# A transformer layer with a mixture of experts: experts' bias added inside its own jobs in the last half, and a new order of the tail

## The chip, the core and the metric

The kernel runs on one core of a Trainium2 chip. The engines named below are PE (TensorE, matrix products), PEld (its weight loads), DVE (VectorE), ACT (ScalarE), POOL (GpSimd) and SP (SyncE, which issues most transfers). The metric is the device time in microseconds. Three runs of the kernel before gave 788.24, 789.04 and 795.55 us, median 789.04 us. The profiled execution took 789.42 us, of which 787.6 us are its span, from the first to the last instruction.

## What is computed

The input is x of 4 batches, 1024 rows and 128 features; there are 16 heads of 8 features. Everything is float32. Cut to what matters:

```
x  = x + attention1(layernorm(x))                  # strictly causal, softmax of att * mask
n  = layernorm(x)
c  = attention2(rope(n)) @ out_proj_w.T + out_proj_b   # causal
x1 = layer_norm(n + c, ln1_w, ln1_b)
gates = softmax(x1 @ gate_w.T + gate_b)            # 8 experts
top 2 of the gates, not renormalised
e_i = x1 @ expert_w[i].T + expert_b[i]
moe = sum over the top 2 of gate_i * e_i
out = x + layer_norm(x1 + moe, ln2_w, ln2_b)
```

## The kernel before

**Tiling.** A batch is cut in two halves of 512 rows, a half in four tiles of 128 rows. Work named `p1` prepares the first attention of a batch, `p2` finishes it and prepares the second attention, `p3` finishes the second attention of a half and does the experts. In the names, `("p3", b, "e0", t)` is a piece of work: t is a tile (0 to 7) for `e0`, `e1` and `moe`, and a half (0 or 1) otherwise.

**Order.** A planner in the file, `schedule()`, fixes the order of all pieces at build time from tables of assumed durations (`JOB_TIMES`, `TURN_TIMES`). It fills three lists: BEFORE (ahead of the attention), DURING (between the attention's score and value products, by far the largest part) and AFTER (behind the last value product). Every engine walks through the same lists and executes its own share in that order, waiting on semaphores, so an early piece that has to wait holds up every later one on its engine. Pieces with a PE part are called jobs. In AFTER, jobs go round over seven PSUM banks, and PE may run ahead of the readers by up to seven jobs.

**What is in AFTER.** The rest of the first half of the last batch (tiles 0 to 3) and all of the last half (tiles 4 to 7), here called the lone half, `LAST_HALF = (1, B - 1, 1)`:

- `num` turns the numerators of one group of heads, `att` divides by the sums, `att_turned` turns the quotient (ACT copies it out), `out` is the output projection, and DVE adds the residual.
- `stats`, `root`, `centre`, `scale`: first normalisation of four tiles. DVE does the moments, the centring and the scaling, POOL the inverse root (L1535, L1536).
- `x1T` turns x1; `gate` is the gate product; `exp` and `pick0` to `pick3` make the matrix G of gates on DVE (with one exponential on ACT).
- `e0` and `e1`: the experts' products of one tile, 512 columns each. In AFTER, ACT multiplies a product by the gates (L1464) and DVE only passes on the semaphore, by `read_by_act`; for the `e0` jobs of the lone half DVE multiplies itself (L1627, `probs<-scores,G`). After `e1`, DVE adds the two (L1627, `psum<-probs`), and POOL's `moe` folds the sum in two steps and adds `x1b` (L1561 to L1563).
- `GT` turns G, and `bias` multiplies it by the 8 rows of experts' biases; DVE adds x1 to make `x1b`. `moe` waits for it.
- `x2` prepares the residual; `stats2`, `root2`, `centre2`, `scale2`, `store`: second normalisation of four tiles and one transfer of 256 KB.

A float32 product of 512 columns shows up in the trace as two PE instructions, and `e0` or `e1` is one such product, so two instructions.

`read_by_act` (in words): DVE waits until ACT has read the job's bank, and then counts the job as free. Banks are freed in the order of the jobs, so PE sees a job as read only when DVE has come to it in its own list.

## Time and profile before

| | us |
|---|---|
| median of three runs | 789.04 |
| profiled execution | 789.42 |
| its span | 787.6 |
| PE busy | 681.1 (86% of the span) |
| ACT busy | 648.1 (82%) |
| DVE busy | 395.9 (50%) |
| POOL busy | 322.9 (41%) |

Shares over the span say little about the last 50 us. There the attention is over, each engine is busy for only part of the time, and the end is set by a chain that goes back and forth between DVE, PE, ACT and POOL. The granted clock of PE is 1.00 or 0.50 of full speed in each stretch (2.4 and 1.2 GHz). Idle time of an engine off the chain costs nothing. Times given as 7xx.xx are positions in the span of the profiled execution.

### The profile page before, as it was taken

Reading aid. Unit: us, or ns where it says so; the run is one execution under the profiler, and the core shown is the slowest. Engines: PE = TensorE matmul, PEld = TensorE weight load, DVE = VectorE, ACT = ScalarE, POOL = GpSimd, SP = SyncE. Lnnn points to the kernel's source line nnn. Section 1 sums busy time; section 2 is a strip of 40 time slices with the busy share of each in tenths; the row PEclk is TensorE's granted clock in tenths of the full one; section 3 lists DMA queues with packets and bytes.
Section 4 is the critical chain, followed back from the end, with each engine's and each line's share of the span. In section 5 each row is a group of like instructions: output and inputs, shape, how many; then the busy total and the mean of one; then the engine's idle time right before and its main releaser. Section 6 shows DMA issues by size and latency. Waiting matters only on the chain. (4 is left out here: it accounts for less than half of the span.)

```text
span 787.6 us, 15418 instructions
## 1 busy us (share of the span) xinstructions
PE 681.1 (86%) x5568; PEld 259.9 (33%) x5568; DVE 395.9 (50%) x1062; ACT 648.1 (82%) x721; POOL 322.9 (41%) x635
## 2 busy tenths in 40 slices
PE   4798998988899989989897989989999789999853
PEld 2333333433234333233232333233333233233422
DVE  5355344456445453556244644574345765455573
ACT  1499997999899997999698889998889798888721
POOL 3162235323633434434553245532666314424334
PEclk9589998999999997999898999999999999999976
DMA  6848357535567432424455244423545451230100
GB/s 162 288 136 263 101 202 239 178 127 202 181 213 243 162 110 86 148 83 135 143 163 155 104 141 130 146 83 121 190 151 179 158 162 60 70 96 1 41 13 15
DMA packets 77142, 109.86 MB, mean 139 GB/s; under 512 B 13928, under 2 KB 28400, under 8 KB 77040
## 3 DMA queue, kind: packets, MB, share of 16 engines
q1 hardware_dynamic: 72944, 107.32, 42.8%
q10 hardware_dynamic: 4096, 1.33, 0.8%
q8 instruction: 46, 0.75, 0.4%
q14 instruction: 56, 0.46, 0.2%
HBM read 60.94 MB, written 47.68 MB: 138 GB/s over the span
## 5 line engine op out<-in xcount | busy, mean ns | idle before, releaser
L1504 ACT ACTIVATE probs<-scores,shift 128x1024 f32<-128x1024 f32 x576 | 601.4, 1124 | 80.2 <-PE scores L1309 73.7
L1580 POOL TENSOR_SCALAR_AFFINE_SELECT probs<-probs 128x256 f32<-128x256 f32 (+1 forms) x448 | 197.5, 458 | 379.8 <-ACT probs L1504 379.1
L1334 PE MATMUL acc<-probs,v 128*9 128x512 f32 (+3 forms) x3072 | 322.2, 508 | 10.7 <-ACT num L1429 9.5
L1309 PE MATMUL scores<-qs,ks 32*128 32x512 f32 (+3 forms) x1536 | 185.1, 434 | 41.0 <-ACT probs L1504 37.4
L1309 PEld LDWEIGHTS scores<-qs,ks 32*128 32x128 f32 x1536 | 83.1, 189 | 259.9 <-ACT probs L1504 175.0
L1334 PEld LDWEIGHTS acc<-probs,v 128*9 128x9 f32 x3072 | 59.1, 100 | 132.2 <-issue 72.9
L1627 DVE TENSOR_TENSOR prod<-side,G 128x512 f32<-128x512 f32 x48 | 33.1, 691 | 89.3 <-PE side L1275 79.3
L1275 PE MATMUL side<-we,x1T 128*128 128x512 f32 x100 | 58.6, 669 | 0.8 <-DVE x1T L1916 0.8
L1561 POOL TENSOR_TENSOR moe<-psum 128x256 f32<-128x256 f32 x32 | 24.4, 762 | 51.3 <-DVE x1b L1627 26.6
L1429 ACT ACTIVATE num<-acc 128x512 f32<-128x512 f32 x64 | 38.2, 596 | 5.3 <-PE acc L1334 5.2
L1536 POOL TENSOR_TENSOR rstd<-rstd,expo 128x4 f32<-128x4 f32 x32 | 33.4, 1044 | 2.7
L1660 DVE COPY xT<-side 128x512 f32<-128x512 f32 x22 | 15.2, 691 | 30.2 <-PE side L1148 30.1
L1675 DVE TENSOR_SCALAR part<-side,binqk 128x512 fp32r<-128x512 f32 x16 | 12.0, 751 | 31.4 <-PE side L1154 21.8
L1154 PE MATMUL side<-xT,win 128*128 128x512 f32 x32 | 20.1, 712 | 6.6 <-DVE part L1676 6.6
L1464 ACT ACTIVATE probs<-scores,G 128x128 f32<-128x128 f32 x40 | 11.0, 389 | 15.4 <-PE scores L1275 9.9
L1675 DVE TENSOR_SCALAR part<-side,bqk 128x512 fp32r<-128x512 f32 x12 | 9.0, 751 | 25.0 <-PE side L1154 25.0
L1635 DVE BATCH_NORM_STATS2 stats<-xrow 128x6 f32<-128x128 f32 x72 | 15.6, 279 | 11.8 <-DMA xrow<-in_x 9.5
L1275 PEld LDWEIGHTS side<-we,x1T 128*128 128x128 f32 x100 | 15.5, 195 | 16.1 <-issue 11.4
L1627 DVE TENSOR_TENSOR psum<-prod 128x512 f32<-128x512 f32 x24 | 17.7, 737 | 3.1
L1275 PE MATMUL scores<-we,x1T 128*128 128x512 f32 x28 | 17.4, 767 | 0.0
L1562 POOL TENSOR_TENSOR moe<-moe 128x128 f32<-128x128 f32 x32 | 15.8, 493 | 2.5
L1848 DVE TENSOR_SCALAR sfx<-side,sfx 128x128 f32<-128x128 f32 x28 | 9.8, 351 | 12.6 <-PE side L1235 8.4
(186 smaller groups left out, 602.4 us busy)
## 6 DMA issues: line engine op xcount, KB each, us to landing
ks<-k_dram SPq DMA_DIRECT2D x96, 256.0 KB, 4.1
q_dram<-part SPq DMA_DIRECT2D x64, 256.0 KB, 3.5
qs<-q_dram SPq DMA_DIRECT2D x64, 256.0 KB, 3.2
num_dram<-num SPq DMA_DIRECT2D x60, 256.0 KB, 3.3
k_dram<-part SPq DMA_DIRECT2D x30, 256.0 KB, 4.0
xrow<-in_x SPq DMA_DIRECT2D x16, 256.0 KB, 4.4
nat<-num_dram SPq DMA_DIRECT2D x15, 256.0 KB
rdenb<-rden_dram SPq DMA_DIRECT2D x15, 256.0 KB
```

What stands on the lines that cost most here:

```text
L1154: signal(pe.matmul(out[:, :], w[:, int(name == "k"), :], xT[a][:, a or j, :], start=True, stop=True), last)
L1275: signal(pe.matmul(out[:, :], x1T[i // TH][:, i % TH, :], we[:, first:first + HALF], start=True, stop=True), last)
L1309: ins = pe.matmul(dst, ks[u][r, kt // TH, (kt % TH) * P:(kt % TH + 1) * P], qs[u][r, q0:q0 + w], start=True, stop=not shifted)
L1334: ins = pe.matmul(acc[h * VW:h * VW + VC, q0:q0 + w], v9[V_OF[k]][:, kt, :, HG * hg + h], src, start=(s == 0), stop=last, skip_group_check ...
L1429: act.activation(num[gp % 2][:, :], acc[:, :], ACT.Copy).then_inc(acc_read, 1)
L1504: act.activation(dst, src, ACT.Exp, bias=shift[:, column(st):column(st) + 1], scale=SCALE).then_inc(probs_raw, 1)
L1536: pool.tensor_tensor(r, r, expo[:, 0:1].broadcast_to(list(r.shape)), ALU.pow).then_inc(root_ready[w], 1)
L1561: link(pool.tensor_tensor(moe[:, :, :], psum4[:, i % 2, 0:2, :], psum4[:, i % 2, 2:4, :], ALU.add))
L1562: link(pool.tensor_tensor(moe1[:, :], moe[:, 0, :], moe[:, 1, :], ALU.add))
L1580: ins = pool.affine_select(out=blocks, in_=blocks, compare_op=ALU.is_ge, fill=0.0, base=a - 1, pattern=[[0, blocks.shape[1]], [1, P]], cha ...
L1627: return dve.tensor_tensor(out, in0, in1, op)
L1675: link(dve.tensor_scalar(pt[:, c, 0, :], src, bias[:, c:c + 1], None, ALU.add))
```

## The change

BEFORE and DURING come out the same; only AFTER changes, and one more transfer is in the loads of weights. In parts:

1. **Bias inside the jobs.** In the lone half `GT` and `bias` are gone. Each of its eight `e0` and `e1` jobs gets a second product, a row of ones (one partition) by a row of 512 bias values, accumulated in the same bank. POOL's last addition takes x1 in place of `x1b`. A tile `be_row` of 4 KB in one partition holds the biases and is loaded with the weights.
2. **Numerators first.** While a `num` job is pending, the planner lets PE take no other job.
3. **Products in two places.** The products of a tile lie in `probs0` or `probs1` by the tile's parity. The `e0` job of tiles 6 and 7 (and in the code that of tile 5 as well: `i > TH`) waits for the sum of the tile but one, no longer for that of the tile before it.
4. **Second normalisation by pairs.** `stats2` to `store` of the lone half are split in A (tiles 4, 5) and B (tiles 6, 7), each with a transfer of 128 KB.
5. The planner models ACT's time of reading otherwise and may let DVE take other work first. This moves rows, too.

```diff
@@ all_turns @@
-        out[x("GT")] = [x("pick3"), x("bias", 1)]
-        out[x("bias")] = [x("GT"), last("moe", 2)]
+        if not alone:
+            out[x("GT")] = [x("pick3"), x("bias", 1)]
+            out[x("bias")] = [x("GT"), last("moe", 2)]
...
+            n = 2 if alone and t > TH else 1
+            out[("p3", b, "e0", t)] = [x("pick3"), ("p3", *((b, "e1", t - n) if t else (b - 1, "e1", T - 1)))]
...
+        if alone:
+            for c, t in (("A", TH + 1), ("B", TH + 3)):
+                out[x("stats" + c)] = [("p3", b, "moe", t)]
+                out[x("root" + c)] = [x("stats" + c)]
+                out[x("centre" + c)] = [x("stats" + c)]
+                out[x("scale" + c)] = [x("centre" + c), x("root" + c), x("x2")]
+                out[x("store" + c)] = [x("scale" + c)]
@@ schedule, behind the last point @@
-            x = next((x for x in pending if x[2] in PIECES and operands(x, t)), None)
+            nums = any(y[2] == "num" for y in pending)
+            x = next((x for x in pending if x[2] in PIECES and (x[2] == "num" or not nums) and operands(x, t)), None)
...
-            if begun and begun[0][1] <= t and ready(begun[0][0], t, NPOINT) and (x is None or left(begun[0][0]) > left(x)):
+            act = acts(begun[0]) if begun and by_act(begun[0][0]) else t
+            if begun and begun[0][1] <= t and ready(begun[0][0], t, NPOINT) and (x is None or (left(begun[0][0]) > left(x) and act <= t + 0.3)):
@@ SP @@
+                if name in ("storeA", "storeB"):
+                    n = 2 * b + i
+                    c = "AB".index(name[-1])
+                    sp.wait_ge(y_ready, n + 1 + c)
+                    ts = slice(2 * c, 2 * c + 2)
+                    sp.dma_start(rows_of(out_d, *rows_half(b, i))[:, ts, :], y_of(n)[:, ts, :]).then_inc(y_out[i], 16)
@@ PE @@
-                        signal(pe.matmul(out[:, :], x1T[i // TH][:, i % TH, :], we[:, first:first + HALF], start=True, stop=True), last)
+                        alone = (1, b, i // TH) == LAST_HALF
+                        ins = pe.matmul(out[:, :], x1T[i // TH][:, i % TH, :], we[:, first:first + HALF], start=True, stop=not alone)
+                        if alone:
+                            ins = pe.matmul(out[:, :], ones[0:1, :], be_row[:, first:first + HALF], start=False, stop=True)
+                        signal(ins, last)
@@ POOL, moe @@
-                        pool.wait_ge(side_free, done(("p3", b, "bias", i // TH)))
+                        if alone:
+                            pool.wait_ge(rows_ready[2], 2 * b + i // TH + 1)
+                        else:
+                            pool.wait_ge(side_free, done(("p3", b, "bias", i // TH)))
+                        added = (x1_of(2 * b + i // TH) if alone else x1b[i // TH])[:, i % TH, :]
@@ DVE @@
-                                dve.wait_ge(products_ready, b * T + i)
+                                dve.wait_ge(products_ready, b * T + i - ((1, b, i // TH) == LAST_HALF and i > TH))
+                    if name[-1] in "AB":
+                        c = "AB".index(name[-1])
+                        ts = range(2 * c, 2 * c + 2)
+                        if name[:-1] == "stats":
+                            dve.wait_ge(moe_ready, b * T + TH * i + 2 * c + 2)
+                            moments(3, y_of(n), 1, ts)
```

**PE, behind the first normalisation of the lone half.** `x1T1` is x1 of the lone half, `x1T0` that of the half before it, `G1` the lone half's gates. Before:

```order
L1275 MATMUL scores<-we,x1T0 128x512 x4
L1251 MATMUL scores<-ident,xrow0 128x128 x4
L1275 MATMUL side<-we,x1T0 128x512
L1257 MATMUL scores<-wg,x1T1 128x8 x4
L1275 MATMUL scores<-we,x1T1 128x512 x4
L1263 MATMUL scores<-ident,G1 8x128 x4
L1270 MATMUL side<-be,GT 128x128 x4
L1275 MATMUL scores<-we,x1T1 128x512 x4
```

And of the change, from the same place (the pair of L1310 and L1313 stands eight times in all; two are shown):

```order
L1310 MATMUL scores<-we,x1T0 128x512 x3
L1285 MATMUL scores<-ident,xrow0 128x128 x4
L1310 MATMUL scores<-we,x1T0 128x512
L1291 MATMUL scores<-wg,x1T1 128x8 x4
L1310 MATMUL side<-we,x1T0 128x512
L1310 MATMUL scores<-we,x1T0 128x512
L1310 MATMUL scores<-we,x1T1 128x512
L1313 MATMUL scores<-be_row,ones 128x512
L1310 MATMUL scores<-we,x1T1 128x512
L1313 MATMUL scores<-be_row,ones 128x512
```

Two experts' jobs of tile 3 moved from ahead of the gate product to behind it, the two rows of turned gates and bias are gone, and the eight jobs behind have twice the products.

**DVE, from the gate logits to the gates of the lone half.** `y` with `l2w` or `x2r` is the second normalisation of the half before it. Before:

```order
L1627 TENSOR_TENSOR gr<-gr 128x32
L1635 BN_STATS stats3<-y 128x6 x4
L1638 BN_AGGR mv3<-stats3 128x2 x4
L1627 TENSOR_TENSOR gmask<-gr,bars8 128x32
L1646 SCALAR_TENSOR_TENSOR y<-y,mv3,l2w 128x128 x4
L1990 TENSOR_REDUCE gsum<-ga 128x4
L1991 RECIPROCAL gsum<-gsum 128x4
L1627 TENSOR_TENSOR gmask<-ga,gmask 128x32
L1627 TENSOR_TENSOR G1<-gmask,gsum 128x32
L1652 SCALAR_TENSOR_TENSOR y<-y,rstd3,x2r 128x128 x4
```

Of the change:

```order
L1674 TENSOR_TENSOR gr<-gr 128x32
L1674 TENSOR_TENSOR gmask<-gr,bars8 128x32
L2050 TENSOR_REDUCE gsum<-ga 128x4
L2051 RECIPROCAL gsum<-gsum 128x4
L1674 TENSOR_TENSOR gmask<-ga,gmask 128x32
L1674 TENSOR_TENSOR G1<-gmask,gsum 128x32
```

The second normalisation of the earlier half left this place.

**DVE, the end of the program.** `xrow0` is the lone half's result. The last rows before:

```order
L1627 TENSOR_TENSOR psum4<-probs1 128x512
L1635 BN_STATS stats3<-xrow0 128x6 x4
L1638 BN_AGGR mv3<-stats3 128x2 x4
L1646 SCALAR_TENSOR_TENSOR xrow0<-xrow0,mv3,l2w 128x128 x4
L1652 SCALAR_TENSOR_TENSOR xrow0<-xrow0,rstd3,xrow 128x128 x4
```

Of the change:

```order
L1674 TENSOR_TENSOR psum4<-probs1 128x512
L1699 SCALAR_TENSOR_TENSOR y<-y,rstd3,x2r 128x128 x4
L1693 SCALAR_TENSOR_TENSOR xrow0<-xrow0,mv3,l2w 128x128 x2
L1699 SCALAR_TENSOR_TENSOR xrow0<-xrow0,rstd3,xrow 128x128 x2
L1682 BN_STATS stats3<-xrow0 128x6 x2
L1685 BN_AGGR mv3<-stats3 128x2 x2
L1693 SCALAR_TENSOR_TENSOR xrow0<-xrow0,mv3,l2w 128x128 x2
L1699 SCALAR_TENSOR_TENSOR xrow0<-xrow0,rstd3,xrow 128x128 x2
```

Between the last sum of products and the last moments there now stand eight instructions: the earlier half's scaling, and pair A's centring and scaling.

## Rows read from the trace of the kernel before

**Rows 1.** Chain that ended last, its end: start, duration in us, engine and work.
```profile
779.04 0.69 POOL moe L1561
...
780.82 0.88 DVE stats L1635 x4
...
781.72 0.39 DVE mv L1638 x4
...
783.79 0.35 DVE xrow L1652
```

**Rows 2.** Timeline, first part of the tail: start, us, engine, line, work [idle before].
```profile
739.29 0.31 DVE L1778 COPY tot<-scores 128x144 f32<-128x144 f32 x1 [3.77 <-ACT probs L1464]
...
745.23 0.69 DVE L1627 TENSOR_TENSOR xrow<-scores,xr 128x512 f32<-128x512 f32 x1
...
747.17 0.86 DVE L1635 BATCH_NORM_STATS2 stats<-xrow 128x6 f32<-128x128 f32 x4
...
750.70 2.14 DVE L1652 SCALAR_TENSOR_TENSOR xrow<-xrow,rstd,l1b 128x128 f32<-128x128 f32 x4
...
750.86 0.77 POOL L1561 TENSOR_TENSOR moe<-psum 128x256 f32<-128x256 f32 x1 [0.36 <-DVE psum L1627]
```

**Rows 3.** Timeline of PE from the last idle stretches on, same columns.
```profile
744.13 3.60 PE L1275 MATMUL scores<-we,x1T 128*128 128x512 f32 x8
...
752.98 1.09 PE L1251 MATMUL scores<-ident,xrow 128*128 128x128 f32 x4 [5.26 <-DVE xrow L1652]
753.86 1.91 PE L1275 MATMUL side<-we,x1T 128*128 128x512 f32 x2
755.57 1.72 PE L1257 MATMUL scores<-wg,x1T 128*128 128x8 f32 x8
757.14 5.82 PE L1275 MATMUL scores<-we,x1T 128*128 128x512 f32 x8
...
768.84 2.04 PE L1270 MATMUL side<-be,GT 8*128 8x128 f32 x8 [3.78 <-DVEq L1624]
770.82 5.82 PE L1275 MATMUL scores<-we,x1T 128*128 128x512 f32 x8
```

**Rows 4.** Stretches: busy us of each engine, granted PE clock, DMA share, GB/s.
```profile
36.00:44.00 8.00, 7.93 (x56) 2.23 (x56) 3.94 (x20) 6.57 (x8) 4.93 (x11) 0.50 0.69 204
...
761.00:762.00 1.00, 1.00 (x3) 0.28 (x3) 0.97 (x7) 0.00 (x0) 0.00 (x0) 0.77 0.00 0
```

**Rows 5.** Timeline of DVE from the logits to the gates, same columns as Rows 2.
```profile
757.79 0.18 DVE L1627 TENSOR_TENSOR gl<-scores,bg 128x32 f32<-128x32 f32 x1
...
760.89 0.87 DVE L1635 BATCH_NORM_STATS2 stats<-y 128x6 f32<-128x128 f32 x4
...
762.29 1.15 DVE L1646 SCALAR_TENSOR_TENSOR y<-y,mv,l2w 128x128 f32<-128x128 f32 x4
...
764.13 0.19 DVE L1627 TENSOR_TENSOR G<-gmask,gsum 128x32 f32<-128x32 f32 x1
...
764.35 1.14 DVE L1652 SCALAR_TENSOR_TENSOR y<-y,rstd,x2r 128x128 f32<-128x128 f32 x4
```

**Rows 6.** Timeline of the end, same columns.
```profile
776.67 1.14 ACT L1464 ACTIVATE probs<-scores,G 128x128 f32<-128x128 f32 x4 [0.90 <-PE scores L1275]
...
778.04 0.69 DVE L1627 TENSOR_TENSOR psum<-probs 128x512 f32<-128x512 f32 x1 [0.56 <-DVEq L1624]
...
784.96 0.39 SPq L1077 DMA_DIRECT2D out_rows<-xrow  x1
```

**Rows 7.** Transfers by name: times issued, KB each, median us to landing.
```profile
rden_dram<-den SPq DMA_DIRECT2D x15, 32.0 KB, 1.6
...
out_rows<-xrow SPq DMA_DIRECT2D x1, 256.0 KB, 2.2
```

**Rows 8.** Timeline of SP near the start, same columns as Rows 2.
```profile
8.84 1.38 SPq L1085 DMA_DIRECT2D count<-in_count  x1
...
17.84 2.77 SPq L1004 DMA_DIRECT2D q_dram<-part  x4
```

More of the change, by code:

```diff
@@ L409, in operands @@
             before = [y for y in waits[x] if y[2] in ("e0", "e1")] + [(*x[0:2], "bias", (x[3] - 2) // TH)]
[L410 removed]
+            if any(y not in jobs for y in before if y in waits or y in done):
                 return False
@@ L531, in left, with acts @@
         return way[x]
+    def acts(begun_job):
+        x, end = begun_job
+        needs = [y for y in waits[x] if y[2] in ("pick3", "e1", "GT")]
+        needs += [("p3", x[1], "pick3", x[3] // TH)] if x[2] in ("e0", "e1") else []
+        return max([clock["ACT"], end] + [done.get(y, 0.0) for y in needs]) + (1.2 if x[2] in ("e0", "e1") else 0.65)
     pending.sort(key=left, reverse=True)
```

50 lines of the change are left out of this document (32 added, 18 removed).

## The prediction

> **What bounds the kernel now.** I read the page's chain and shares first. PE is busy for 86% of the span and ACT for 82%, but both in the attention, whose order the change doesn't touch. All that differs lies in the last 50 us. So I asked the timeline of those 50 us which wait ends last at each step, and the chain of waits for the very end.
>
> Three stretches show up. Up to 752.84, DVE leads: numerators, quotient, residual and first normalisation of the lone half. The numerators' copy at 739.29 had DVE idle for 3.77 us, ended by ACT's multiplication of an expert's product that stands ahead of it in DVE's list; the scaling at 750.70 takes 2.14 us and ends at 752.84 [rows 2]. From 752.98 to 764.3 it is PE, then DVE, that lead: turned x1, gate product, and the gates, ready at 764.13 + 0.19 = 764.32 [rows 3, 5]. Behind it the bias product has to wait for DVE to come to the turned gates in its list, starts only at 768.84, and four jobs follow it until 776.64 [rows 3]. Then the last sum of products, two rounds of POOL's `moe`, the moments at 780.82, the scaling and the transfer [rows 1, 6].
>
> PE's clock matters here. Eight expert instructions took 3.60 us at 744.13, about 0.43 us from one start to the next with 0.6 for the last; at 757.14 eight took 5.82 us [rows 3]. PE had been idle for 5.26 us before 752.98, and in the stretch 761 to 762 the granted clock is 0.77, a mix of the two levels (1.2 and 2.4 GHz); it rose at 761.46, since 0.54 of that microsecond at 1.00 and 0.46 at 0.50 give 0.77 [rows 3, 4]. At the lower level an expert instruction costs 0.86 us from start to start (two of them: 753.86 to 755.57, 1.71 us) [rows 3].
>
> **The change, step by step.** Positions are on the clock of the profiled execution.
>
> *Numerators first.* PE turns them before the first expert's job, and DVE's copy no longer stands behind ACT's reading. It waits only for PE, at about 738.4 in place of 739.29: 0.9 earlier [rows 2]. Ahead of the moments, before, from the residual's start to theirs took 747.17 - 745.23 = 1.94 us, with a sum of products between them that waited for ACT. Now `x1b` of the earlier half stands there: 0.69 twice less overlap, about 1.4 us. So the moments start about 1.4 earlier, at 745.8. Behind them DVE now does two things ahead of the scaling (residual's bias and a sum, 0.69 each, about 1.4 with waits) where it had one: 0.5 is given back. The scaling starts at 749.8 in place of 750.70, takes the same 2.14, and PE turns x1 at 752.1: **0.9 earlier** [rows 2, 3]. POOL's root isn't late: `moe` of tile 0 starts at 745.8, takes 1.8 (779.0 to 780.8) [rows 1], and the root adds 1.4, to 749.0.
>
> *Gate and gates.* PE goes from turned x1 to the instruction behind the gate product in 757.14 - 752.98 = 4.16 us as before, to 756.24 [rows 3]. On DVE two pieces of the earlier half's second normalisation leave the gates' way: moments 0.87 + about 0.38 and centring 1.15 [rows 5]. A wait for ACT's multiplication of tile 3 comes in, about 0.7 us, since that job's product now comes from PE behind the gate product. The gates took 764.32 - 757.79 = 6.53 us from the logits [rows 5]; now 6.53 - 2.4 + 0.7 = 4.8, from 756.9, so they are ready at 761.7 in place of 764.32.
>
> *Expert jobs.* PE has two jobs of tile 3 left, 4 instructions at 0.86 = 3.44 us, to 759.68. Then the eight jobs of the lone half, 16 products before and 32 instructions now. The bias rows cost as much as the weights' columns do: 512 columns pass in either. The gates at 761.7 are in time for the first reader, at about 762.4, and no bank is late, since the gates free them. So **PE leads from 752.1 to the last job**: until 761.46 it does 1.78 / 0.86 = 2 instructions at the lower level, then 29 starts at 0.43 and 0.6 for the last = 13.0 us, which ends at 774.5. Before, it ended at 770.82 + 5.82 = 776.64 [rows 3]: 2.1 earlier. The bias and its wait behind DVE are gone, 16 instructions have come in.
>
> The transfer of the bias row: SP issues one more. Its last weight's issue ends at 10.22 and its next work starts at 17.84 [rows 8]; in those 7.6 us one issue hides, so it is priced at nothing. Without the cover it would be at most the 1.38 of the row.
>
> *The end.* ACT 774.5 + 1.14; 0.23 to DVE's sum (777.81 to 778.04) [rows 6] and 0.69 of it: 776.6. POOL starts `moe` 0.1 later and takes 1.8: 778.5 [rows 1]. Before, the last `moe` began at 779.04 and the moments at 780.82 [rows 1]: so this is 2.3 earlier. But DVE now has eight scalings and centrings between the last sum and pair B's moments. Free of POOL, four take 1.14 (764.35) [rows 5], eight 2.3, to 778.9. Next to a `moe`, four took 2.14 (750.70), 1.0 more, while POOL's first step took 0.77 against the 0.69 of the last `moe` [rows 1, 2]. I take this dearer value, since the same line runs next to the same POOL work: 776.6 + 2.3 + 1.0 + 0.1 = **780.0 for pair B's moments, only 0.8 earlier**. What POOL has done by 778.5 waits for DVE until 780.0. The pair's moments take half (0.87 + 0.38 becomes 0.63), the root about as before (from the moments' end to the scaling 783.79 - 782.11 = 1.68 [rows 1]), the scaling 0.57 in place of 1.14: 782.9 against 784.93. The span ended 2.67 us behind that; SP issued at 784.96 [rows 6]. A transfer of 128 KB in place of 256: from 0 to 0.6 us less (32 KB landed in 1.6, 256 in 2.2) [rows 7]; I take 0.3. The span ends at 782.9 + 2.4 = 785.3.
>
> The Trainium skill (SBUF — State Buffer, section "SBUF: two separate sides") has VectorE and GpSimd arbitrate for a shared port pair that one holds for a whole instruction while the other fully blocks, which covers VectorE instructions with two SBUF inputs. By that rule the eight (2.3) and `moe` (1.7) would run one after the other and pair B's moments would start at about 780.7, the span ending at 786.0. The row is milder: at 750.70, four of these and three of POOL's, 1.14 and 1.7 us of work, shared 2.14 us, so part of it overlapped [rows 2].
>
> **Sum.** 787.6 - 785.3 = 2.3 to 2.4 us off. Against the profiled execution 789.42 - 2.4 = 787.0; the median of the runs, 789.04, lies 0.38 below that execution, so 789.04 - 2.4 = **786.6 us**. A measurement of this kernel can tell about 1% (7.9 us) from no change; this is 0.3%.
>
> **Rivals.**
>
> *The clock stays low (slower).* The attention's start shows PE busy for 7.93 of 8.00 us, 36 to 44, at a granted clock of 0.50 all along [rows 4]: being busy didn't lift it there. Half of the new instructions are products of one row, of which no row shows what they do to the clock. If it stays at 0.50 through the eight jobs, 31 starts at 0.86 + 0.95 from 759.68 end at 787.3, 12.8 later than in my sum: 786.6 + 12.8 = **799.4 us**. The place where it decides: each microsecond at the lower level costs half of one, so at 2.4 us lost, a rise 4.8 us later than 761.46, the gain is zero. Against it: from 756.24 to about 761.4 PE does only full products without a gap, as it did before the rise of 761.46, and it never rests afterwards. 7%.
>
> *DVE and POOL get more in each other's way.* If the two take turns wholly, at the end as above, and POOL's root of pair A (which ends 0.3 before the last `moe` could start) comes late as well, the gain shrinks by 0.7 + 0.6: **787.9 us**. For it: 2.14 against 1.14. 20%.
>
> *They don't.* DVE is done at 778.9 and pair B's moments start behind POOL at 778.9 instead of 780.0, and the transfer gives its 0.6: 1.1 + 0.3 more, **785.2 us**. For it: other scalings of the same shape took 1.14 next to nothing. 18%.
>
> *The reordering does nothing.* If the gates came later than 762.4, DVE would lead again and the freed PE order would be worth little; with the numerators' 0.9 lost as well, about **789 us**. Slack for this is 0.7 us. 7%.
>
> My forecast holds 48%, from 785.9 to 787.3.
>
> **How the numbers follow.** All but the first rival stay within 1% of 789.04. The range goes from 784.2 (the milder end, with 0.5 to 1 us of scatter between runs, as 788.24 and 789.04 show) to 789.6 (the reordering worth nothing, with the same scatter); it leaves out the low clock and some tail, about 13%. Faster by over 1% needs 7.9 us, which no case gives: 2%. Slower by over 1% needs the clock low for nearly all jobs: 6%. Within: 92%.
>
> **What would show it.** Right: the numerators' copy without ACT ahead of it, near 738.4; turned x1 near 752.1; gates near 761.7; a granted clock that rises near 761.5; the last expert instruction ending near 774.5, without idle PE in front; PE at 0.43 from start to start; DVE's eight between 776.6 and 780.0, and pair B's moments released by DVE's own queue rather than by POOL; SP's last issue near 782.9. Wrong: bias instructions longer than 0.43 at the full clock, PE waiting for a bank, a clock at 0.50 past 766, or pair B's moments waiting for POOL.

## The result, and the profile after

| | before | changed |
|---|---|---|
| median of the runs, us | 789.15 | 796.26 |
| profiled execution's span | 787.6 | 797.2 |
| last numerators copied by ACT (start) | 737.00 | 741.52 |
| last scaling of DVE (end) | 784.93 | 794.96 |
| between the two, below "the tail" | 47.9 | 53.4 |

The changed kernel is slower: ratio 1.0079, 95% interval 1.0055 to 1.0103. I had forecast 786.6 us, and up to 789.6. Medians here and below are of all runs, while the ratios leave out runs over 1.5% above a kernel's fastest (at most two of a changed kernel, five of before; e14's profile is of such a run), so a ratio isn't always the quotient of the medians.

Of the 9.6 us between the two spans, 4.5 lie ahead of the tail, where the order of work is the same; they are scatter of single executions (the additional load is tested in e4). In the 17 profiles of this document the tail begins between 730.86 and 745.44, though the order of work up to there is the same in all. The tail took 5.5 us more. Positions of after are therefore 4.52 us later than those I had predicted. PE is busy for longer, as the page's busy row says (86% and 681.1 us before):

```profile
PE 691.3 (87%) x5572; PEld 258.6 (32%) x5572; DVE 394.8 (50%) x1061; ACT 648.2 (81%) x720; POOL 323.1 (41%) x637
```

Most of the path went as said. Timeline of after, DVE and PE, with start, us, engine, line, work, idle before:

```profile
742.93 0.31 DVE L1825 COPY tot<-scores 128x144 f32<-128x144 f32 x1 [2.88 <-PE scores L1231]
...
756.61 1.09 PE L1285 MATMUL scores<-ident,xrow 128*128 128x128 f32 x4 [5.01 <-DVE xrow L1699]
...
766.32 0.19 DVE L1674 TENSOR_TENSOR G<-gmask,gsum 128x32 f32<-128x32 f32 x1
```

The numerators' copy waits for PE alone, at 742.93 - 4.52 = 738.4 (predicted 738.4; [rows 2] has 739.29). PE turns x1 at 752.1 (predicted 752.1; [rows 3] has 752.98). The gates are ready at 766.51 - 4.52 = 762.0 (predicted 761.7; [rows 5] give 764.32).

Then the expert jobs. Timeline of PE; a pair of float32 instructions (x2) is one product of 512 columns. L1310 is the product with the weights, L1313 that of the bias row:

```profile
765.30 1.12 PE L1313 MATMUL scores<-be_row,ones 1*128 1x512 f32 x2
766.35 1.13 PE L1310 MATMUL scores<-we,x1T 128*128 128x512 f32 x2
...
773.73 1.23 PE L1313 MATMUL scores<-be_row,ones 1*128 1x512 f32 x2
774.89 2.07 PE L1310 MATMUL side<-we,x1T 128*128 128x512 f32 x2
...
784.91 2.07 PE L1313 MATMUL scores<-be_row,ones 1*128 1x512 f32 x2
```

Predicted was 0.86 us from one product to the next at the full clock. It is 1.05 (766.35 - 765.30), and from 774.89 on it is 2.00. The last job ends at 786.98, 45.5 us into the tail; before, at 776.64, 39.6 into it. The stretches of 1 us (busy time of PE, PEld, DVE, ACT and POOL with the number of instructions, granted clock, DMA share, GB/s) say what went with the second:

```profile
764.00:765.00 1.00, 1.00 (x3) 0.22 (x1) 0.77 (x2) 0.45 (x2) 0.00 (x0) 0.81 0.00 0
765.00:766.00 1.00, 1.00 (x3) 0.29 (x2) 0.86 (x5) 0.69 (x3) 0.00 (x0) 1.00 0.00 0
...
773.00:774.00 1.00, 1.00 (x3) 0.27 (x2) 0.00 (x0) 0.92 (x4) 0.99 (x1) 1.00 0.07 16
774.00:775.00 1.00, 1.00 (x3) 0.13 (x2) 0.70 (x2) 0.00 (x0) 0.08 (x1) 0.81 0.00 0
775.00:776.00 1.00, 1.00 (x2) 0.39 (x2) 1.00 (x3) 0.00 (x0) 0.92 (x2) 0.50 0.00 0
...
785.00:786.00 1.00, 1.00 (x2) 0.40 (x2) 0.00 (x0) 0.00 (x0) 0.48 (x1) 0.50 0.00 0
```

PE is busy for 1.00 of every microsecond, and yet the granted clock is 1.00 only from 764.38 (0.62 of that microsecond at 1.00 and the rest at 0.50 make 0.81) to 774.62; then it falls back to 0.50, 1.2 GHz, and doesn't rise again. Before, it was 0.77 in the stretch of the rise [rows 4]. Before, too, the clock fell once more, at 768.28 (0.64 in the stretch 768 to 769), and came back at 775.11; but there PE had been idle for 3.78 us ahead of the bias product [rows 3]. Here it has no such pause.

The end, from the last reading by ACT, is as predicted:

```profile
788.38 0.69 DVE L1674 TENSOR_TENSOR psum<-probs 128x512 f32<-128x512 f32 x1 [4.01 <-DVEq L1671]
788.99 2.14 DVE L1699 SCALAR_TENSOR_TENSOR y<-y,rstd,x2r 128x128 f32<-128x128 f32 x4
789.15 0.76 POOL L1608 TENSOR_TENSOR moe<-psum 128x256 f32<-128x256 f32 x1 [3.67 <-DVE psum L1674]
791.05 0.60 DVE L1693 SCALAR_TENSOR_TENSOR xrow<-xrow,mv,l2w 128x128 f32<-128x128 f32 x2
791.69 0.61 DVE L1699 SCALAR_TENSOR_TENSOR xrow<-xrow,rstd 128x128 f32<-128x128 f32 x2
792.22 0.48 DVE L1682 BATCH_NORM_STATS2 stats<-xrow 128x6 f32<-128x128 f32 x2
...
794.35 0.61 DVE L1699 SCALAR_TENSOR_TENSOR xrow<-xrow,rstd 128x128 f32<-128x128 f32 x2 [0.72 <-POOL rstd L1575]
```

From the end of the last job to the end of the last scaling it takes 794.96 - 786.98 = 7.98 us (predicted 8.4, before 8.29). Pair B's moments start at 792.22, when DVE has done its eight; POOL had ended its sum at 790.98.

### The profile page after: what moved, and what is told of

Read it like the earlier page. It is cut to its first block, busy times and chain, and to the rows that moved or that the text cites. A ratio compares the mean times of both kernels' runs of the same rounds, so it can differ in the third digit from the quotient of the medians.

```text
span 797.2 us, 15420 instructions
## 1 busy us (share of the span) xinstructions
PE 691.3 (87%) x5572; PEld 258.6 (32%) x5572; DVE 394.8 (50%) x1061; ACT 648.2 (81%) x720; POOL 323.1 (41%) x637
## 3 DMA queue, kind: packets, MB, share of 16 engines
q1 hardware_dynamic: 72962, 107.32, 42.7%
## 4 chain that ended last, share of the span: by engine, by line
PE 59%; ACT 15%; issue 9%; DVE 6%; POOL 3%; DMA 3%; SPq 1%; ACTq 1%; DVEq 0%; POOLq 0%
PE acc L1373 25%; PE scores L1348 13%; ACT probs L1543 13%; PE side L1310 6%; PE side L1188 4%; ACT num L1468 2%; PE side L1246 2%; PE scores L1310 2%; PE scores L1313 1%; POOL probs L1627 1%; PE side L1182 1%; PE side L1194 1%; ACTq L1520 1%; DMA xrow<-in_x 1%; PE side L1304 1%
## 5 line engine op out<-in xcount | busy, mean ns | idle before, releaser
L1310 PE MATMUL side<-we,x1T 128*128 128x512 f32 x100 | 61.1, 695 | 1.0 <-DVE x1T L1963 1.0
L1575 POOL TENSOR_TENSOR rstd<-rstd,expo 128x4 f32<-128x4 f32 (+1 forms) x33 | 33.9, 1027 | 2.8
L1503 ACT ACTIVATE probs<-scores,G 128x128 f32<-128x128 f32 x40 | 11.2, 377 | 18.6 <-PE scores L1313 12.8
L1310 PEld LDWEIGHTS side<-we,x1T 128*128 128x128 f32 x100 | 16.1, 203 | 18.1 <-issue 12.4
L1310 PE MATMUL scores<-we,x1T 128*128 128x512 f32 x28 | 18.2, 757 | 0.0
L1574 POOL TENSOR_SCALAR rstd<-mv 128x4 f32<-128x4 f32 (+1 forms) x33 | 9.7, 293 | 16.6 <-DVE mv L1685 16.2
```

Source lines behind the costliest of these rows:

```text
L1310: ins = pe.matmul(out[:, :], x1T[i // TH][:, i % TH, :], we[:, first:first + HALF], start=True, stop=not alone)
L1575: pool.tensor_tensor(r, r, expo[:, 0:1].broadcast_to(list(r.shape)), ALU.pow).then_inc(root_ready[w], 1)
```

## The experiments

All measures of the tail come from one profiled execution each, and how late the clock rises in it moves a tail by up to 3.4 us (last section). The tail of e4, whose order is that of before, took 49.6 for 47.9, with a clock at 0.50 from 742.44 to 745.85. So differences of one or two us between tails show nothing by themselves. "15 products" is the time on PE from the start of the first bias product to the end of the last product of the jobs: fifteen of the sixteen, since the first product of all stands ahead. Ratios are against the kernel before, measured beside each.

| run | what | median us | ratio, 95% interval | tail | 15 products |
|---|---|---|---|---|---|
| changed | | 796.26 | 1.0079 [1.0055, 1.0103] | 53.4 | 21.68 |
| e9 | the same again | 794.83 | 1.0043 [1.0006, 1.0079] | 56.4 | 26.90 |
| e10 | before + bias rows only | 798.63 | 1.0108 [1.0045, 1.0171] | 60.3 | 30.11 |
| e1 | 128 rows, loaded | 788.52 | 0.9975 [0.9945, 1.0005] | 44.5 | 13.04 |
| e13 | 128 rows, zeros filled | 781.41 | 0.9875 [0.9836, 0.9914] | 44.5 | 13.03 |
| e6 | 64 rows | 789.59 | 1.0001 [0.9962, 1.0039] | 45.2 | 15.88 |
| e14 | 32 rows | 787.41 | 0.9950 [0.9919, 0.9981] | 45.3 | 15.87 |
| e5 | one row, alternating | 784.48 | 0.9944 [0.9900, 0.9988] | 46.3 | 14.51 |
| e2 | no bias product | 784.80 | 0.9912 [0.9878, 0.9946] | 42.0 | |
| e3 | bias by turned gates | 784.61 | 0.9945 [0.9917, 0.9972] | 44.2 | |
| e4 | before + the load | 788.13 | 0.9985 [0.9951, 1.0018] | 49.6 | |
| e7 | numerators first only | 785.33 | 0.9947 [0.9898, 0.9995] | 45.5 | |
| e8 | pairs only | 788.85 | 0.9995 [0.9954, 1.0037] | 47.6 | |
| e11 | e5, scaling earlier | 784.16 | 0.9921 [0.9883, 0.9959] | 42.7 | 14.51 |
| e12 | e3, root later | 785.05 | 0.9932 [0.9894, 0.9971] | 43.2 | |
| e15 | e13, scaling earlier | 786.00 | 0.9921 [0.9885, 0.9957] | 44.0 | 13.03 |

### e1, e2, e3, e4: which part brings the loss

e1, the row filled up:

```diff
-        be_row = sb("be_row", [1, NE * D])
+        be_row = sb("be_row", [P, NE * D])
...
-                            ins = pe.matmul(out[:, :], ones[0:1, :], be_row[:, first:first + HALF], start=False, stop=True)
+                            ins = pe.matmul(out[:, :], ones[:, :], be_row[:, first:first + HALF], start=False, stop=True)
```

> The changed kernel, but the second product of each expert's job takes all 128 partitions: ones of 128 x 128 by a tile whose row 0 is the bias row and whose other rows are zero. Same columns, same number of instructions, same order, same result. (One transfer is 512 KB in place of 4.) I read a tail, from the start of ACT's last copy of the accumulator to the end of DVE's last scaling: 47.9 us before, 53.4 with the change. Theory A (one-row products cost a weight load that isn't hidden and don't hold the clock up): the starts within a pair of products come 0.43 apart throughout, the granted clock stays at 1.00 to the last expert product, the tail is 46 to 48 us, and the time is within 0.4% of before. Rival B (it is the number of products, or the clock goes down by itself whatever the rows): the clock falls to 0.50 in the middle of the experts' jobs again, starts are 0.53 apart, the tail stays at 52 to 54 and the time 0.8% above before.

e2, the second product left out, so that these tiles lack their experts' bias:

```diff
-                        ins = pe.matmul(out[:, :], x1T[i // TH][:, i % TH, :], we[:, first:first + HALF], start=True, stop=not alone)
-                        if alone:
+                        ins = pe.matmul(out[:, :], x1T[i // TH][:, i % TH, :], we[:, first:first + HALF], start=True, stop=True)
+                        if False:
```

> The changed kernel without the second product of the lone half's expert jobs: these tiles' outputs lack the experts' bias. Everything else, with the order, is as in the change. Both theories: PE has 16 instructions fewer, so 7 to 14 us of work, and DVE or ACT leads from the gates on. If the rows are the whole loss, the tail is 43 to 46 us (before 47.9, change 53.4), and the time 0.3 to 0.6% below before. Rival: if the new order itself is bad (tile 3's jobs behind the gates, eight DVE instructions ahead of the last moments), the tail stays over 48 and the time is at or above before.

e3, each part of the change behind a switch, the bias one off; and e4, to the kernel before:

```diff
+BIAS_IN, NUM_FIRST, TWO_PLACES, BY_PAIRS, ACT_MODEL = False, True, True, True, True
...
-                        alone = (1, b, i // TH) == LAST_HALF
+                        alone = (1, b, i // TH) == LAST_HALF and BIAS_IN
```

> The change with its first part undone: turned gates and the bias product are back for the lone half, numerators first, products in two places, second normalisation by pairs and the planner's model of ACT stay (the planner makes its own order of it). Theory A: the one-row products were the loss, so the tail is 45 to 48 us and the time 0 to 0.4% below before. Rival: the loss is in the other parts; the tail is 50 or more and the time stays about 0.8% above before.

```diff
+        be_row = sb("be_row", [1, NE * D])
...
-(be, be_d), (count, count_d)]
+(be, be_d), (be_row, be_d.rearrange("e d -> (e d)").unsqueeze(0)), (count, count_d)]
```

> The kernel before with nothing but the additional tile of one partition and its load of 4 KB among the weights. The profiled execution of the change had lost 4.5 us ahead of the tail, where the order is the same in both. Theory A (that is the scatter of executions): within 0.15% of before. Rival C (the additional load delays the first loads of x or the stores behind it): 0.3 to 0.6% slower.

The loss is in the one-row products; no other part shows one. Without them (e2, 0.88% below before), or with the turned gates in their place (e3, 0.55%), the rest of the change is a gain; the load (e4) can't be told from nothing. The tails of e1, e2 and e3 all came out 0.8 to 1.5 us below what I had expected, and the times of e2 and e3 too. In e1, the same products in the same order with 128 rows in place of one leave the tail 8.9 us shorter. PE in e1:

```profile
762.30 1.02 PE L1310 MATMUL scores<-we,x1T 128*128 128x512 f32 x2
763.16 1.02 PE L1313 MATMUL scores<-be_row,ones 128*128 128x512 f32 x2
...
771.74 1.02 PE L1313 MATMUL scores<-be_row,ones 128*128 128x512 f32 x2
```

They stand 0.86 us apart and the fifteen take 13.04 us, as my sum had it (13.0), and the granted clock stays at 1.00 to their end (772.76):

```profile
772.00:773.00 1.00, 0.76 (x2) 0.00 (x0) 0.96 (x4) 0.20 (x1) 0.92 (x2) 1.00 0.00 0
```

PE's loads of weights (PEld) in after, and in e1 (below), where a load lies beside the product before it (the one at 763.16 is for the product's second instruction, which starts at 763.59):

```profile
765.30 0.29 PEld L1313 LDWEIGHTS scores<-be_row,ones 1*128 1x128 f32 x2 [0.76 <-issue]
766.35 0.30 PEld L1310 LDWEIGHTS scores<-we,x1T 128*128 128x128 f32 x2 [0.76 <-issue]
```

```profile
763.16 0.19 PEld L1313 LDWEIGHTS scores<-be_row,ones 128*128 128x128 f32 x1 [0.24 <-issue]
763.59 0.19 PEld L1310 LDWEIGHTS scores<-we,x1T 128*128 128x128 f32 x1 [0.24 <-issue]
```

In after PEld idles for 0.76 us ahead of the first load of each product and the load starts with the product itself; in e1 each single load starts 0.24 us behind the end of the one before it, while PE is busy with the instruction ahead. A load itself takes 0.18 to 0.19 us in both, for one row or for 128.

### e5 and e6: the order, and the number of rows

e5, the two products of every second job in the other order, so that row product stands by row product and weights by weights; the work is the same:

```diff
+                        two = [(x1T[i // TH][:, i % TH, :], we[:, first:first + HALF]), (ones[0:1, :], be_row[:, first:first + HALF])]
+                        two = two[:1] if not alone else two[::-1] if JOB[job] % 2 else two
+                        for n, (weights, cols) in enumerate(two):
+                            ins = pe.matmul(out[:, :], weights, cols, start=n == 0, stop=n == len(two) - 1)
```

> The changed kernel with the two products of every second expert job in the opposite order (bias row first, then weights), so that two one-row products of neighbouring jobs stand side by side and the pairs of rows in PE's array change half as often; the work is the same. Theory 'a switch of the array's rows costs the 0.19 us': two instructions of one kind that follow two of the same kind stand 0.86 us apart at the full clock, those behind a switch 1.06, so the sixteen pairs cost 8 x 0.2 = 1.6 us less at the full clock. Theory 'any one-row product is slow by itself': every pair that contains one keeps 1.06. On the clock: if it falls because half of PE's instructions fill one row of 128, it falls here too, 8 to 11 us behind the first one-row product, and the tail (start of ACT's last numerator copy to the end of DVE's last scaling) is 51 to 53 us with a time near 794. If it were the changing itself that lets it fall, it stays at 1.00 and the tail is about 46, the time near 788.

e6, 64 rows:

```diff
-                            ins = pe.matmul(out[:, :], ones[0:1, :], be_row[:, first:first + HALF], start=False, stop=True)
+                            ins = pe.matmul(out[:, :], ones[0:64, :], be_row[:, first:first + HALF], start=False, stop=True)
```

> The changed kernel with 64 rows in the bias product (row 0 the bias, 63 rows of zeros, by 64 rows of ones) in place of one. Theory 'few rows in use let the clock fall': 64 rows are half of the array; if the effect is one of degree, the fall of the clock comes later than in the changed kernel or not at all, with a tail of 44.5 to 48 us (44.5 was with 128 rows, 53.4 with one). If anything short of 128 rows counts as one row does, the clock falls about 10 us behind the first such product and the tail is near 53. On the spacing: if a load of weights isn't hidden whenever the number of rows changes, pairs stand 1.06 apart at the full clock as with one row; if only a one-row load is exposed, 0.86.

PE of e6, then of e5 with the stretch of its last job:

```profile
758.77 1.12 PE L1313 MATMUL scores<-be_row,ones 64*128 64x512 f32 x2
759.82 1.13 PE L1310 MATMUL scores<-we,x1T 128*128 128x512 f32 x2
...
773.53 1.12 PE L1313 MATMUL scores<-be_row,ones 64*128 64x512 f32 x2
```

```profile
761.29 1.98 PE L1313 MATMUL scores<-be_row,ones 1*128 1x512 f32 x4
763.20 1.98 PE L1313 MATMUL scores<-we,x1T 128*128 128x512 f32 x4
...
775.00:776.00 1.00, 0.80 (x2) 0.00 (x0) 0.77 (x5) 0.17 (x1) 0.84 (x3) 1.00 0.00 0
```

On the price of a product this settles it. 64 rows beside 128 cost the same 1.05 us as one row, so few rows aren't what is dear. In e5 four instructions (two products of a kind) take 763.20 - 761.29 = 1.91 us, that is 0.86 + 1.05: the one behind a change of kind costs 0.19 more, the other nothing. In e6 PEld idles for 0.76 us ahead of each product's first load, as in after. So what costs is **the change in the number of rows between neighbours**, 0.19 us each time at the full clock, about the time of one load (0.19 in e1's rows). Fifteen such changes, which I had priced at nothing, are 2.85 us.

The Trainium skill has two statements on this (TensorE: Matmul & The Clock Gate). The section "Step-by-step: what each phase is for" says that loads are pulled ahead of running products if the row groups don't conflict or the load goes to the background buffer, and that a load's time goes by columns, not by rows. The second holds here (0.18 to 0.19 us for one row as for 128); whether the load is pulled ahead did hang on the rows of the two neighbours. The sentence in "The mechanism" that a load overlaps a running product only where the row group differs doesn't fit: with equal rows (e1) the load is hidden, and with 64 beside 128 (e6) it isn't.

On the clock, each of the two theories fails in one of the two runs. By the share of one-row work the clock of e5 should have fallen; it stayed at 1.00 from 760.34 to behind the last product (0.83 in the stretch from 760), with a tail of 46.3 as the other theory, the changing itself, had it. But e6 changes its rows as often as after does, and with 64 rows the clock didn't fall. So neither the share of one-row work nor the changing does it alone. The times fit the tails only roughly: e6's median is that of before (ratio 1.0001, within 0.4%), though its tail was 2.7 us shorter.

### e9 and e10: is it the rows, and is it always so

e9 is the changed kernel once more. e10 is the kernel before with the bias rows alone (the switches of e3 as `True, False, False, False, False`).

> The changed kernel once more, on the chip of the next three, for a second profile of its tail. Theory 'its expert products let the clock fall': the granted clock is 0.50 again for the later expert jobs with PE busy throughout, about 10 us behind the rise, and the tail is 51 to 54 us (53.4 in the first profile). Rival 'the fall was an accident of that one execution, and the time is lost elsewhere': the clock stays at 1.00 and the tail is 46 to 47.5, that of the alternating order (46.3) and the 1.06 us spacing, while the time stays near 796.

> The kernel before with one part of the change: the experts' bias by one-row products within the lone half's jobs, no turned gates and no bias product; numerators, reading places and second normalisation as before. Theory 'this part alone brings the loss': the clock falls to 0.50 among the last jobs while PE is busy, the tail is 51 to 54 us against 47.9 of before, the time 3 to 7 us above before. Rival 'the loss needs the reordering too (PE without any rest from x1T on)': before, DVE's gates come later, so PE rests ahead of the jobs and the clock's rise comes later; then the tail is 47 to 49 and the time within 1.5 us of before.

Of e9:

```profile
753.00:754.00 1.00, 1.00 (x7) 0.80 (x5) 0.00 (x0) 0.56 (x3) 0.00 (x0) 0.61 0.00 0
754.00:755.00 1.00, 1.00 (x6) 0.75 (x7) 0.18 (x1) 0.58 (x3) 0.00 (x0) 1.00 0.00 0
...
760.00:761.00 1.00, 1.00 (x3) 0.30 (x2) 0.73 (x2) 0.69 (x3) 0.00 (x0) 0.80 0.00 0
761.00:762.00 1.00, 1.00 (x3) 0.16 (x1) 0.83 (x2) 0.45 (x2) 0.72 (x1) 0.50 0.00 0
...
781.87 2.07 PE L1313 MATMUL scores<-be_row,ones 1*128 1x512 f32 x2
```

Of e10, two stretches and the first and last row product:

```profile
746.00:747.00 1.00, 0.00 (x0) 0.00 (x0) 1.00 (x3) 0.00 (x0) 0.84 (x3) 0.59 0.00 0
747.00:748.00 1.00, 0.26 (x2) 0.29 (x3) 1.00 (x3) 0.00 (x0) 0.44 (x1) 0.50 0.00 0
...
753.88 2.07 PE L1319 MATMUL scores<-be_row,ones 1*128 1x512 f32 x2
...
781.92 2.07 PE L1319 MATMUL scores<-be_row,ones 1*128 1x512 f32 x2
```

In e9 the clock rises at 753.78, and falls at 760.60, 3.6 us behind the first row product (757.04). In e10 it falls at 746.18 in the pause of PE ahead of turned x1 and **never rises**: PE is busy without a gap from 747.74 to 783.99, for 36 us, at 0.50. Its first 6.1 us hold no row product, and in the kernel before, too, the rise came only 8.5 us behind the same pause; the 30 us behind 753.88 are those of the row products. So neither the reordering nor an accident is needed. Both losses were larger than I had expected (tails 56.4 and 60.3 for 51 to 54).

Three profiles alone wouldn't rule an accident out, but every run has its mean granted clock on record. Over the whole span its median is 0.938 in the 20 runs of the change, 0.940 in the 8 of e9 and 0.934 in the 4 of e10, and 0.942 to 0.945 in the runs of before beside the experiments; in the seven kernels whose bias products have more rows or alternate (e1, e5, e6, e11, e13 to e15) it is 0.9445 to 0.9605.

The Trainium skill (same page, section "What's actually happening") has a gate set by how busy PE has been. By the rows here PE's busy share was 1.00 from the first row product to the last, in after, e9 and e10 as in e5 and e6; so the busy share of a profile doesn't tell on which side the gate falls.

### e7 and e8: where the rest of the change gains

Both are the kernel before with one part switched on (`False, True, False, False, True`, and `False, False, False, True, False`).

> The kernel before with one part of the change: numerators of the lone half ahead of the experts' first job, with the new planning of ACT's reads; turned gates and their bias product as before, second normalisation whole. Theory 'the path to x1T is what the change gained': my sum had 0.9 us for the numerators and up to 1.7 us more from what moves out of the way of the gates; so the tail is 45.5 to 47 us (47.9 before), the time 1 to 2.5 us below before. Rival 'the gain of e3 (tail 44.2) is in the pairs at the end': the tail here stays at 47.5 or more and the time equals before.

> The kernel before with one part of the change: the second normalisation of the lone half in two pairs of tiles, all else as before. Theory of the sum: the pair's moments, scaling and transfer save 0.6 + 0.6 + 0.3 at the end, and pair A's root now stands on POOL ahead of the last expert sum; so 0.5 to 1.5 us less in the time, tail 46.5 to 47.5 us. Rival 'the gain of e3 is in the pairs': a tail near 44.5 and the time 3 to 4 us lower. Rival 'pair A's root delays the last sum on POOL': no gain, tail near 48.

e7 has most of e3's gain: PE turns x1 15.09 us into the tail (755.37 - 740.28) where it was 15.98, the predicted 0.9; its last job ends 36.7 into it where it was 39.6. Its time is 4.2 us below before by the ratio (interval 0.4 to 8.1), where I had expected 1 to 2.5. e8 gets 0.4 us of tail, less than the 0.5 to 1.5 expected, and nothing that the runs can tell; its last job ends at 39.8, as before. In e8 pair A's root holds POOL from 772.42 to 773.89, while DVE's last sum has been there since 773.00 and POOL's last sum of experts starts at 773.86; e12 takes this up.

### e11, e12: the end

e11 is e5 with the earlier half's last scaling and its transfer directly behind that half's centring:

```diff
+behind([("scale2", 0), ("store", 0)], ("centre2", 0))
```

> The kernel of e5 (the two products in alternating order) with the earlier half's last scaling (four instructions on DVE) and its transfer put directly behind that half's centring, instead of behind the last sum of products. My sum said that pair B's moments wait for eight scalings and centrings of DVE, of which four run at 2.14 us beside POOL's expert sum; in e5 these moments started at 781.05, 1.25 us behind POOL's last sum (779.80). Theory: without the four they start right behind POOL's sum, so the tail is 45.0 to 45.3 in place of 46.3, the time 1 us lower. Rival 'DVE gets no faster, it only does the four elsewhere and is late with a sum of products': the tail stays at 46 or more. Since the clock's rise differs from one execution to the next by some microseconds, the stretch from the last job's end on PE (e5: 775.80, to the last scaling's end 783.79 = 7.99) is the surer number: 6.7 to 7.0 by the theory, 8.0 by the rival.

e12 is e3 with pair A's root behind the last sum of POOL, and pair B's moments ahead of pair A's scaling:

```diff
+behind([("rootA", 1), ("statsB", 1), ("scaleA", 1), ("storeA", 1)], ("moe", 7))
```

> The kernel of e3 (all of the change but the experts' bias, which stays with the turned gates) with pair A's root on POOL behind the last expert sum instead of ahead of it, and pair B's moments on DVE ahead of pair A's scaling. In e3 POOL worked on the root from 778.09 to 779.15 and began the last expert sum at 779.13, though DVE's sum had been there since 777.82. Theory: the last sum starts about 1.0 us earlier, the root of pair A then stands between that and pair B's, so 0.8 to 1.1 us less: tail 43.1 to 43.4 (44.2), time 783.5 to 784 and below both kernels. Rival 'pair A's scaling and transfer become the last': no gain, tail 44.2 or more.

(`behind` takes the named pieces out of the list AFTER and puts them behind the last one named.) The end of e11, DVE and POOL:

```profile
774.47 1.07 DVE L1704 SCALAR_TENSOR_TENSOR xrow<-xrow,mv,l2w 128x128 f32<-128x128 f32 x2
774.63 0.76 POOL L1619 TENSOR_TENSOR moe<-psum 128x256 f32<-128x256 f32 x1 [0.55 <-DVE psum L1685]
775.47 0.46 POOL L1620 TENSOR_TENSOR moe<-moe 128x128 f32<-128x128 f32 x1
775.57 1.03 DVE L1710 SCALAR_TENSOR_TENSOR xrow<-xrow,rstd 128x128 f32<-128x128 f32 x2
776.00 0.45 POOL L1621 TENSOR_TENSOR xrow<-moe,xrow 128x128 f32<-128x128 f32 x1
776.53 0.47 DVE L1693 BATCH_NORM_STATS2 stats<-xrow 128x6 f32<-128x128 f32 x2
```

Pair B's moments start 0.08 us behind POOL's last sum (776.45), where in e5 it was 1.25. From the last product's end (772.46) to the last scaling's end (779.26) it takes 6.80 us in place of 7.99, as the theory said (6.7 to 7.0). So the step of the prediction that DVE's eight hold up pair B's moments is shown. The whole tail is 3.6 us shorter, of which this is 1.2; the rest is an earlier rise of the clock (754.56 against 760.34 in e5), which is another execution's, not the edit's. The time, 784.16, can't be told from e5's 784.48, where I had expected 1 us less. Here two centrings and two scalings beside POOL took 1.07 and 1.03 us, where two alone take 0.61 (794.35 in after). A narrower window of the same timeline shows the second of the centrings by itself:

```profile
774.73 0.81 DVE L1704 SCALAR_TENSOR_TENSOR xrow<-xrow,mv,l2w 128x128 f32<-128x128 f32 x1
```

It takes 0.35 us where POOL rests, and here lasts until 775.54, 0.15 behind the end of POOL's step (775.39); the two scalings end 0.15 behind POOL's next two steps in the same way, and these take 0.46 and 0.45, no more than with DVE idle (0.46 and 0.45 at 779.80 and 780.33 in before). So it is DVE that waits, and POOL is hardly slowed. Where DVE starts first it is the other way round: in before, DVE's sum starts at 778.04 and takes its usual 0.69, and POOL's last step, started at 778.11, takes 0.93 in place of 0.45. The Trainium skill (SBUF — State Buffer, section "SBUF: two separate sides") has VectorE, in instructions with two SBUF inputs, and GpSimd share a port pair: the one that starts first holds it for its whole instruction, and the other blocks. The trace agrees, by these ends. The overlap that the prediction saw in the 2.14 us at 750.70 comes from DVE needing only 0.15 us behind POOL's step, not its full 0.35.

In e12 the root no longer stands ahead of the last sum:

```profile
774.53 0.77 POOL L1625 TENSOR_TENSOR moe<-psum 128x256 f32<-128x256 f32 x1
...
776.33 0.23 POOL L1591 TENSOR_SCALAR rstd<-mv 128x2 f32<-128x2 f32 x1
```

The tail is 43.2, as expected (43.1 to 43.4) and 1.0 below e3; behind the last product it takes 9.76 us where e3 took 10.71. The times of e3 and e12, 0.9945 and 0.9932 of before, can't be told apart, where I had expected 783.5 to 784 us and less than e3's.

### e13, e14, e15: by degree, the load, and a version to keep

By now 128, 64 and one row were known. e13 is e1 with the zeros written by POOL at the start and 4 KB loaded in place of 512; e14 the same with 32 rows; e15 is e13 with e11's edit.

```diff
-FIRST_FILLS = NVB + 3
+FIRST_FILLS = NVB + 4
...
+                if d is WEIGHTS[-2][1]:
+                    sp.wait_ge(filled, FIRST_FILLS)
...
-                     + [(v9[i][:, :, :, :], 1.0) for i in range(NVB)])
+                     + [(v9[i][:, :, :, :], 1.0) for i in range(NVB)] + [(be_row[:, :], 0.0)])
```

> As e1 (bias product with 128 rows, row 0 the bias and 127 of zeros), but the zeros are written by POOL at the start and only the bias row is loaded (4 KB in place of 512 KB). Theory 'the large load costs some us in the body': tail as in e1, 44.5 us, within 1 (the moment of the clock's rise differs by some us from one execution to the next), and a time of 784.5 to 786.5, 2 to 4 below e1's. Rival 'the load costs nothing, e1's median was scatter': the time is 787 to 789.5 as e1's.

> The changed kernel with 32 rows in the bias product (row 0 the bias, 31 of zeros written at the start). Theory 'by degree': 32 rows of 128 lie between one (clock falls 6 to 10 us behind its rise, tail 53 to 60) and 64 (stays at 1.00, tail 45.2). If the clock falls as with one row, the tail is 53 or more and the time near 796; if it stays, the tail is 45 to 46.5 and the time 786 to 788, and only products of fewer rows do it. On spacing both say 1.06 us a pair, since the number of rows changes between neighbours as with 1 and 64.

> e13 with the earlier half's last scaling and its transfer directly behind that half's centring, as e11 did to e5. Theory 'DVE's eight stand between the last sum and pair B's moments': from the end of the last expert product on PE to the end of the last scaling 7.0 us in place of 8.0 (e1: 772.76 to 780.75 = 7.99), tail 43.5, time 783.5 to 785.5, about 1 below e13 and below every kernel but e11. Rival 'moved, not removed': 8.0 again and e13's time.

PE of e14 and the stretch in which its last product ends:

```profile
766.90 1.12 PE L1315 MATMUL scores<-be_row,ones 32*128 32x512 f32 x2
...
781.65 1.12 PE L1315 MATMUL scores<-be_row,ones 32*128 32x512 f32 x2
...
782.00:783.00 1.00, 0.77 (x2) 0.00 (x0) 0.35 (x3) 0.19 (x1) 0.92 (x3) 1.00 0.00 0
```

32 rows behave as 64 do: 1.05 us a product and a clock that stays up. Of the sizes tried, only one row lets it fall. e13 is the fastest by its (six) runs, 1.25% below before (interval 0.86 to 1.64%), with e1's tail to the tenth (44.5). Its median lies 7.1 us below e1's, more than the 2 to 4 that I had expected of the smaller load. The runs' clocks speak against the load as the cause of most of it. The two profiled executions have nearly the same mean clock (0.952 and 0.950) and the same span (783.0), with the last numerators at 736.23 and 736.19; and e13's six runs simply had a higher clock, median 0.9605, against 0.9445 in e1's twelve and 0.9495 in e15's, which have e13's small load and 786.0. So the 1.25% can't be put down to the filled rows alone; why the clock differs over whole executions isn't known. In e15 the end from the last product took 7.22 us (778.67 to 785.89) in place of 7.99, 0.8 of the 1.0 expected; its time wasn't lower than e13's and lay above the 783.5 to 785.5 expected. Between these versions the runs' scatter is larger than the edits.

## Why the prediction was wrong

**The step that failed** is this one: "The bias rows cost as much as the weights' columns do: 512 columns pass in either", with its 0.43 us from start to start and, behind it, the argument against the low clock, that PE "never rests afterwards". It missed two things, and the runs part them. The fifteen products took 21.68 us where the sum had 13.0, which is what e1 and e13 take (13.04, 13.03):

- Price of a product: 15.88 in e6 and 15.87 in e14, whose clock stays at 1.00, less 13.03: **2.85 us** for the changes of rows.
- Clock: 21.68 - 15.88 = **5.8 us** (11.0 in e9, 14.2 in e10).

Together 8.65, and 0.8 comes back since the clock rose 1.6 us earlier than I had put it (764.38 - 4.52 = 759.86, not 761.46): 7.9 us. The last job ended at 786.98 - 4.52 = 782.46, 8.0 later than the predicted 774.5. That the clock rose within 1.6 us of my 761.46 is luck: I had taken over the moment of a single execution, and behind turned x1 the rise came anywhere from 2.7 to 9.4 us. Over both profiles the tail is 54.9, which is 7.0 above the 47.9 of before, and the medians differ by 7.1.

**The rivals.** "The clock stays low" named the right mechanism and said which row was missing: what one-row products do to the clock. Its price was 12.8 us for a clock that never rises in the jobs; e10 has that (and 14.2 us, since a change of rows costs more at the low clock, 2.00 in place of 1.71 us a product), after and e9 part of it. I gave it 7%, on the strength of a clock that rose before and a PE without rest. The first was the state ahead of the row products, the second no protection: e10 was never idle from turned x1 on. With 36 to 44 us at 0.50 and PE busy for 7.93 of 8 [rows 4] I had a row that said so, and gave it too little weight. I also hadn't asked what PE did there: products of 32 rows (scores) in turn with products that fill 9 columns (`acc<-probs,v`), none of them a full one. That alone doesn't keep the clock low, since from 44.66 on the same kinds, with some full products between them, run at 1.00; but it was a stretch without full products, and my argument against the rival was about full ones. The breaking point, too, was in hand: each us at the low level costs half of one, and the gain of 2.4 is gone after 4.8.

**What held.** Numerators 738.4, turned x1 752.1, gates 762.0 for 761.7: within 0.3. In e7 the numerators' part gains the 0.9 at turned x1. "PE leads from 752.1 to the last job" held. The end held in its size (7.98 against 8.4) and its reason (e11). The pairs gained less by themselves (0.4) than I had thought, since pair A's root holds up POOL (e12). The load was rightly nothing (e4). Where the row products do cost what I had put (e1, e13), the medians are 788.5 and 781.4, one above and one below my 786.6; the tails of these, 44.5, lie 1.4 below my 45.9 (782.9 - 737.0); 1.0 of it is the clock, which rose 22.5 us into the tail of e1 (at 758.70) and not 24.5.

## What to carry over

A small product that is squeezed between large ones isn't priced by its columns: if its number of rows differs from its neighbour's, a load of weights comes into the open (0.19 us here each time at the full clock), so put like beside like, or fill it up with zeros to the rows of its neighbours. And a row of the profile in which PE is busy doesn't promise its full clock: where a stretch holds an instruction of a kind that no stretch before had, price it at both levels of the clock, and give the lower one a chance to match.

## What was not expected of the hardware

- With one-row products between full ones PE's granted clock fell from 1.00 to 0.50 with PE busy for 1.00 of each microsecond (774.62 in after, and 760.60 in e9), or stayed at 0.50 through 36 us of unbroken work (e10). With 32, 64 or 128 rows in the same order it stayed at 1.00 to the last product.
- The same one-row products in alternating order didn't let it fall (e5, e11). What tells the orders apart is that a product takes 0.95 us on average in place of 1.05, and which neighbours it has; which of these decides was not tried. The average alone doesn't, since 64 and 32 rows have 1.05, too.
- Behind the pause of PE of some 5 us ahead of turned x1, the rise came 2.7 us behind PE's next instruction in e6 (752.57 to 755.26), 7.8 in after, 8.5 before and 9.4 in e7 (755.37 to 764.76), in kernels whose order up to there is much alike. Half of such a difference is time: up to 3.4 us between executions, more than most edits of the tail are worth.
